# Routing of the second expert stage moved into retention; shared tiles and expert blocks in one program

## The chip, the cores and the metric

The kernel runs on one core of one Trainium2 chip. The metric is the device time of one execution in microseconds, the median of the runs. A core has TensorE (PE, matrix products), VectorE (DVE), ScalarE (ACT), GpSimd (POOL) and SyncE (SP, which here only issues transfers). Each engine works through its own instruction list in order, and they meet at semaphores.

## What is computed

4096 tokens (16 sequences of 256) with 128 channels pass through six residual stages:

```python
    x = x + 0.5 * _L0_ffn_ref(_layernorm(x, axis=-1), ...)
    x = x + _L0_attn_ref(_layernorm(x, axis=-1), ...)
    x = x + 0.5 * _L0_ffn_ref(_layernorm(x, axis=-1), ...)
    x = x + 0.5 * _L1_ffn_ref(_layernorm(x, axis=-1), ...)     # experts, first time
    x = x + _L1_attn_ref(_layernorm(x, axis=-1), ...)          # retention, 8 heads
    x = x + 0.5 * _L1_ffn_ref(_layernorm(x, axis=-1), ...)     # experts, second time
    return x
```

Retention projects q, k, v and a gate, rotates q and k, multiplies the scores by a fixed decay instead of a softmax, normalises each head's output, gates it and projects it back. The expert stage:

```python
        topk_idx, tw = _route(x, router_w, bias)   # sigmoid, 2 of 4 groups by their two best, 4 of 16 experts
        combine = (jax.nn.one_hot(topk_idx, E, dtype=tw.dtype) * tw[..., None]).sum(1)
        h = jnp.einsum('td,edf->etf', x, gate_w)
        u = jnp.einsum('td,edf->etf', x, up_w)
        y = jnp.einsum('etf,efd->etd', jax.nn.silu(h) * u, down_w)
        routed = jnp.einsum('etd,te->td', y, combine)
        sh = jax.nn.silu(x @ sh_gate_w) * (x @ sh_up_w) @ sh_down_w   # shared experts, every token
        return (routed + sh).reshape(hidden_states.shape)
```

## The kernel before

The residual `x_res` stays in SBUF as 32 tiles of 128 tokens. The stages are separate programs (`nc.Block`), one after the other. In each, every engine has a list that code writes out; there is no scheduler.

**Retention** (`retention_phase`) works in 64 steps, a pair of heads of one sequence each, so four steps make a sequence. `software_pipeline` is given, for each engine, its operations with a lead: in step s an operation with lead 3 works on pair s + 3. The order in that list is the order in the step. It runs as a loop on the engines, except for its first and last steps. PE does in a step: scores, projection of q and k (`project_qk`), `retain` (decayed scores by values), `project_v` (into the bank `ps_b`), `transpose_heads`, `project_gate`, `project_out`. Once a sequence it transposes the next one's normalised x (`transpose_x`, L1743, also into `ps_b`). DVE does: `shift_of_head`, `decay`, `turn` (L1615, rotation products), `head_statistics`, `gate_heads` (z, L1645); and for a sequence the split of x, residual, normalisation (L1601), statistics, and the adding back of the first expert stage's rows. POOL adds the rotated halves (`rotate`, L1669), without which the next scores can't start.

**The second expert stage** is `moe_phase`: `moe_route`, then `moe_blocks`, both 32 tiles or 37 blocks long and written out.
`moe_route` first runs through all 32 tiles in groups of four: statistics on DVE, inverse deviation on POOL, normalisation on ACT (into `rows`), transposes and router products on PE. Then come 32 tiles of the shared experts (`gate_up`, silu on ACT, `multiply` on DVE at L626, `transpose_act`, `down`; once in four tiles DVE's `add_shared` (L632) empties the bank that `down` fills). Between the multiplications DVE works on the choice of experts (`topk`), for 16 tiles of tokens at a time, four small operations after each tile:

```python
            for s in range(SEGS):
                for i in range(0, TOPK, 4):
                    topk(s, i, i + 4)
                    shared(done, done + 1)
                    done += 1
                classes(s)
                weights_of_row(s)
```

PE counts the rows of each class (`rank_tokens`), POOL scatters each tile's rows to DRAM (`slots`, L679), and DVE fills a table of blocks. `moe_blocks` then takes 37 blocks of 128 rows that share a pair of expert groups, computes their eight experts, and scatters the results (`y_rows`), which are read back and added at the end.

## Time and profile before

| what | value |
|---|---|
| three runs | 1536.6 us median, 1534.93 to 1537.35 |
| the profiled execution | 1533.22 us, of which the span in the trace is 1531.4 us |
| busy in the span | PE 88%, DVE 63%, ACT 52%, POOL 40% |
| mean granted TensorE clock | 0.943 of full speed |

The profile is of one execution. "Busy" counts the engine's computing; an engine that holds at a semaphore is idle. Behind an arrow stands what ended the idle time before an instruction. Retention fills about 775 to 1185 us of the span, the second routing and shared tiles 1185 to 1299 us, the second blocks 1300 to 1513 us.

### The profile page before, as it was taken

The page shows a single profiled execution, that of the slowest core. Times are in us where ns is not written, and L with a number is a line of the kernel's source. Part 1 is how long each engine was busy: PE and PEld are TensorE (multiplying, and loading weights), DVE is VectorE, ACT ScalarE, POOL GpSimd, SP SyncE. Part 2 cuts the span into 40 slices and gives each one's busy share as a digit, 9 for nine tenths or more (in the row PEclk, how much of TensorE's full clock was granted, in tenths as well). Part 3 has the DMA queues.
Part 4 walks back from the last instruction along what each step waited for, and adds up shares of the span by engine and source line. Part 5 has one row for each costly group of instructions (what it writes and reads, how often), then busy time and mean ns, then how long its engine had stood idle before and what let it go on. Part 6 is the DMA issues. An engine that isn't in the chain of part 4 may idle for free. (4 is left out here: it accounts for less than half of the span.)

```text
span 1531.4 us, 36438 instructions
## 1 busy us (share of the span) xinstructions
PE 1349.6 (88%) x10678; PEld 1139.4 (74%) x10678; DVE 968.9 (63%) x3998; ACT 790.5 (52%) x1899; POOL 609.3 (40%) x905
## 2 busy tenths in 40 slices
PE   6799999999766679999969999999997766999994
PEld 5577777776754568888858888888887445888884
DVE  6467777775766735555547777777776683555553
ACT  2267777777244234444336666666665622344441
POOL 2177777776250622222124444444443244111111
PEclk9899999999658899999979999999999788999998
DMA  5399300000220100000012121111210001000004
GB/s 142 87 296 277 104 0 0 0 1 2 98 88 17 45 30 25 27 27 25 23 49 49 47 51 48 46 48 48 51 41 22 1 31 34 24 27 25 27 27 121
DMA packets 101068, 81.59 MB, mean 53 GB/s; under 512 B 10060, under 2 KB 88591, under 8 KB 100704
## 3 DMA queue, kind: packets, MB, share of 16 engines
q1 hardware_dynamic: 95162, 68.82, 16.7%
q0 software_dynamic: 4416, 9.58, 1.8%
q10 hardware_dynamic: 1382, 1.83, 0.4%
q8 instruction: 58, 0.95, 0.3%
q14 instruction: 50, 0.41, 0.1%
HBM read 22.67 MB, written 40.75 MB: 41 GB/s over the span
## 5 line engine op out<-in xcount | busy, mean ns | idle before, releaser
L912 DVE SCALAR_TENSOR_TENSOR moe_block_act<-banks,moe_taken,moe_block_gated 128x128 f32<-128x128 f32 x592 | 166.8, 344 | 188.7 <-ACT moe_block_gated L956 180.7
L941 POOL DMA_INDIRECT y_rows<-moe_block_y,moe_taken x74 | 71.3, 963 | 366.5 <-ACT moe_block_y L966 366.5
L1231 POOL TENSOR_TENSOR attn_z<-attn_top,attn_z 128x256 f32<-128x256 f32 x256 | 155.7, 617 | 60.1 <-DVE attn_top L1178 60.1
L1178 DVE CUSTOM_DVE_ANT_0 attn_z<-banks,rel_bias 128x128 f32<-128x128 f32 (+1 forms) x512 | 148.5, 352 | 42.2 <-PE banks L1326 40.8
L956 ACT ACTIVATE moe_block_gated<-banks 128x512 f32<-128x512 f32 x148 | 88.6, 599 | 160.4 <-PE banks L997 160.3
L1669 POOL TENSOR_TENSOR ret_rotated<-ret_turned 128x512 f32<-128x512 f32 x64 | 82.1, 1283 | 189.5 <-DVE ret_turned L1615 189.5
L1013 PE MATMUL banks<-moe_down,moe_block_actT 128*128 x1184 | 156.3, 275 | 0.0
L1013 PEld LDWEIGHTS banks<-moe_down,moe_block_actT 128*128 128x128 f32 x1184 | 143.8, 192 | 0.3
L995 PE MATMUL banks<-moe_hi,moe_block_x_hi 128*128 x296 | 130.9, 442 | 1.7 <-DVE moe_block_x_lo L902 1.5
L1712 ACT ACTIVATE ret_normed<-banks,ret_head_shift,ret_head_rstd 128x128 f32<-128x128 f32 x256 | 96.4, 457 | 56.7 <-DVE ret_head_shift L1639 56.7
L1264 ACT ACTIVATE attn_prob<-banks 128x384 f32<-128x384 f32 x256 | 119.2, 492 | 7.2 <-PE banks L1336 2.4
L997 PE MATMUL banks<-moe_hi,moe_block_x_lo 128*128 x296 | 118.2, 399 | 0.0
L996 PE MATMUL banks<-moe_lo,moe_block_x_hi 128*128 x296 | 117.9, 398 | 0.0
L1336 PE MATMUL banks<-ident,attn_z 128*128 128x128 f32 x768 | 109.1, 278 | 0.7 <-ACT attn_prob L1264 0.7
L679 POOL DMA_INDIRECT slots<-moe_rows,moe_row_i x64 | 62.7, 979 | 106.1 <-issue 53.9
L1336 PEld LDWEIGHTS banks<-ident,attn_z 128*128 128x128 f32 x768 | 84.3, 141 | 14.4 <-issue 13.9
L1004 PE MATMUL banks<-ident,moe_block_act 128*128 128x128 f32 x592 | 89.1, 273 | 0.0
L1732 PE MATMUL banks<-ret_x_hi,ret_hi 128*128 128x256 f32 x256 | 84.5, 330 | 0.9 <-DVE ret_x_lo L1608 0.9
L1004 PEld LDWEIGHTS banks<-ident,moe_block_act 128*128 128x128 f32 x592 | 71.7, 141 | 17.1 <-DVE moe_block_act L912 0.2
L1615 DVE TENSOR_TENSOR ret_turned<-ret_twins,ret_cos_sin 128x1024 f32<-128x1024 f32 x64 | 77.8, 1215 | 6.1 <-DMA ret_twins<-ret_twins 6.0
L1621 DVE TENSOR_TENSOR ret_decayed<-banks,ret_decay 128x768 f32<-128x768 f32 x64 | 61.2, 956 | 30.6 <-PE banks L1788 29.9
L1645 DVE TENSOR_TENSOR ret_z<-ret_affine,ret_gate 128x512 f32<-128x512 f32 x64 | 44.3, 693 | 55.1 <-ACT ret_affine L1721 55.1
(264 smaller groups left out, 3637.5 us busy)
## 6 DMA issues: line engine op xcount, KB each, us to landing
slots<-moe_pad SPq DMA_DIRECT2D x12, 2304.0 KB, 19.9
ret_twins<-ret_twins SPq DMA_DIRECT2D x256, 64.0 KB, 2.0
moe_taken<-slots SPq DMA_DIRECT2D x74, 72.0 KB, 1.8
moe_stage<-in_moe_w SPq DMA_DIRECT2D x4, 576.0 KB, 6.6
bias_reversed<-scratch SPq DMA_DIRECT2D x1, 2048.0 KB, 9.9
back_of_seq<-y_rows SPq DMA_DIRECT2D x16, 128.0 KB, 2.2
moe_back<-y_rows SPq DMA_DIRECT2D x8, 256.0 KB, 4.9
out<-x_res SPq DMA_DIRECT2D x8, 256.0 KB, 4.2
```

What stands on the lines that cost most here:

```text
L912: last = dve.scalar_tensor_tensor(act_f[:, i, at], ps_u[:, i, at], taken[:, b % RB, column:column + 1], gated[:, i, at], ALU.mult, ALU.mult)
L956: act.activation(gated[:, k % 2, :], ps_h[:, k % 2, :], ACT.Silu).then_inc(gated_ready, 1)
L995: pe.matmul(out, hi, w_hi[:, bass.ds(at, HALF)], start=True, stop=False)
L996: pe.matmul(out, hi, w_lo[:, bass.ds(at, HALF)], start=False, stop=False)
L997: pe.matmul(out, lo, w_hi[:, bass.ds(at, HALF)], start=False, stop=True).then_inc(ready, 1)
L1004: last = pe.transpose(ps_a[:, i, e * P:(e + 1) * P], act_f[:, i, e * P:(e + 1) * P], ident[:, :])
L1013: last = pe.matmul(ps_y, actT[:, i, e * P:(e + 1) * P], w["down"][:, bass.ds(at + e * C, C)], start=(i == 0 and e == 0), stop=(i == 1 and ...
L1178: last = dve.tensor_tensor_reduce(out=z[:, s, cols], in0=ps_s[:, i, cols], in1=bias, scale=1.0, scalar=-3.0e38, op0=ALU.add, op1=ALU.max, ...
L1231: pool.tensor_tensor(z[:, s, P:WIDTH], top[:, s, 1:2].to_broadcast([P, WIDTH - P]), z[:, s, P:WIDTH], ALU.subtract).then_inc(shifted1, 1)
L1264: act.activation(prob[:, slot(k, i), :], ps_p[:, i % 2, 0:WIDTH], ACT.Exp, scale=-1.0).then_inc(prob_ready, 1)
L1336: last = pe.transpose(ps_p[:, i % 2, j * P:(j + 1) * P], z[:, s, j * P:(j + 1) * P], ident[:, :])
L1712: last = act.activation(normed[:, r, i, :], ps_o[:, r, i * RET_V:(i + 1) * RET_V], ACT.Identity, bias=head_shift[:, r, i:i + 1], scale=hea ...
```

## The change

A class `RouteFront` holds the routing of the second stage. Its work is now put between the operations of retention, behind the sequence that it needs: in step 4(q+1) the statistics of sequence q (whose residual is then complete), inverse deviation on POOL and, one step later, the normalisation, now on POOL too; two steps after that the transposes on PE, and two further on the router. Router logits come straight out with tokens on partitions (`x_hi` as the stationary operand, 16 columns), so the transposes of logits go. The choice is made for 10, 12 and 10 tiles: the first in steps 26 to 39, the second in steps 50 to 59, the third in the shared tiles. A segment is now 48 operations on DVE, each waiting for the one before. 14 of the 32 scatters are issued on POOL in retention. Front operations on PE use `ps_b` too, so `project_v` waits until they are read out.

Retention is written out in full (`every_step`) instead of looped. Its `turned` tile is gone: the products are written over `twins`, and the copy of q and k waits for `rotated_ready` instead of `turned_ready`. The `retire` (clearing of semaphores and a barrier) that stood between retention and the second expert stage now stands before retention.

`moe_tail_phase` is one program for the 32 shared tiles and the 37 blocks. It transposes and splits the stored normalised rows again for the shared experts, a group ahead. The last sequence's front and the last segment's choice run among its tiles.

```diff
+FRONT_SEGMENTS = ((0, 10), (10, 12), (22, 10))
+class RouteFront:
+    RANK_AT, ROW_AT, OPS = 35, 43, 48
...
+    def normalise(self, pool, q):
+        pool.wait_ge(self.rstd_done, q + 1)
+        for j in range(BATCH_TILES):
+            t = q * BATCH_TILES + j
+            last = pool.tensor_scalar(self.rows[:, t, 0:C], self.x_res[:, t, :], self.mv[:, q % 2, j, 0:1], self.rstd[:, q % 2, j:j + 1],
+                                      ALU.subtract, ALU.mult)
+        last.then_inc(self.xn_ready, 1)
...
+    def router(self, pe, q, ps):
+        r_hi, r_lo = self.w["router"]
+        pe.wait_ge(self.x_split, q + 1)
+        for j in range(BATCH_TILES):
+            hi, lo = self.x_hi[:, j * P:(j + 1) * P], self.x_lo[:, j * P:(j + 1) * P]
+            out = ps[:, j * MOE_E:(j + 1) * MOE_E]
+            pe.matmul(out, hi, r_hi, start=True, stop=False)
+            pe.matmul(out, hi, r_lo, start=False, stop=False)
+            last = pe.matmul(out, lo, r_hi, start=False, stop=True)
+        last.then_inc(self.routed, 1)
...
 def retention_phase(...)
+    RANKS = {40: 0, 60: 1}
+    SIGMOIDS = {25: 0, 49: 1}
+    CHOICES = {0: (26, 40), 1: (50, 60)}
+    SCATTERS = {step: (step - 42,) for step in range(42, 52)} | {62: (10, 11), 63: (12, 13)}
...
-                wait_free(dve, rotated_ready, pair(it, k, 2))
-                dve.tensor_tensor(turned[:, k % 2], twins[:, k % 2], w["cos_sin"][:, :, :].unsqueeze(2).to_broadcast(shape), ALU.mult).then_inc(turned_ready, 1)
+                dve.tensor_tensor(twins[:, k % 2], twins[:, k % 2], w["cos_sin"][:, :, :].unsqueeze(2).to_broadcast(shape), ALU.mult).then_inc(turned_ready, 1)
...
+            every_step(-9, STEPS, U, [
+                (1, shift_of_head), (0, front_statistics), (3, decay), (0, front_choice(0)), (0, front_aggregate), (6, per_seq(0, split_x)),
+                (0, front_split), (0, front_rows), (4, turn), (0, front_choice(1)), (2, head_statistics), (0, front_choice(2)),
+                (1, gate_heads), (0, front_choice(3)),
                 (0, per_seq(RET_PAIRS - 1, residual)), (7, per_seq(0, normalise_x)), (8, per_seq(0, layernorm)), (9, per_seq(0, add_back))])
...
+            every_step(-8, STEPS, U, [
+                (4, rotate), (2, inverse_head_std), (8, per_seq(0, inverse_std)), (0, front_std), (0, front_normalise), (0, front_scatter)])
...
+            every_step(-6, STEPS, U, [
+                (1, normalise_heads), (6, per_seq(0, copy_x_hi)), (0, front_copy), (5, copy_plain), (5, copy_value), (1, scale_heads), (3, silu_gate),
+                (0, front_sigmoid)])
...
@@ project_v
+                step = it * U + k - 5
+                if step % 4 == 3 and step >= 7:
+                    pe.wait_ge(front.x_split, (step - 7) // 4 + 1)
+                if step % 4 == 1 and step >= 9:
+                    pe.wait_ge(front.logits_ready, (step - 9) // 4 + 1)
...
+            every_step(-6, STEPS, U, [
+                (0, front_job), (6, per_seq(0, transpose_x)), (3, scores), (5, project_qk), (2, retain), (5, project_v), (1, transpose_heads),
                 (3, project_gate), (0, project_out)])
...
+def moe_tail_phase(...):
+            for t in range(TILES):                       # DVE
+                g = t // GROUP
+                multiply(t)
...
+                if t % GROUP == 1 and 2 <= g + 1 < GROUPS:
+                    split_x(g + 1)
+                if t % GROUP == 2 and t > GROUP:
+                    add_shared(g - 1)
+                if 4 <= t < RANK_TILE:
+                    front.choose(dve, LAST, (t - 4) * 4, (t - 3) * 4)
+                elif t == RANK_TILE:
+                    front.choose(dve, LAST, (t - 4) * 4, front.OPS, ps_rank)
```

On DVE, in retention, this is what a step holds. Before, a step of the loop in which the next sequence's x is normalised (`shift_of_head` at L1639 to z at L1645, then `ret_xn`):

```order
L1639 SCALAR_TENSOR_TENSOR ret_head_shift<-ret_head_mv,ret_head_rstd 128x4
L1619 REGISTER_ALU
L1621 TENSOR_TENSOR ret_decayed<-banks,ret_decay 128x768
L1615 TENSOR_TENSOR ret_turned<-ret_twins,ret_cos_sin 128x1024
L1627 BN_STATS ret_head_stats<-banks 128x6 x4
L1632 BN_AGGR ret_head_mv<-ret_head_stats 128x2 x4
L1527 REGISTER_ALU
L1645 TENSOR_TENSOR ret_z<-ret_affine,ret_gate 128x512
L1601 TENSOR_SCALAR ret_xn<-x_res,ret_mv,ret_rstd 128x128 x2
```

After, DVE again, step 50, the first of the second segment's choice (tiles are named `front_`; 192 elements are 12 tiles of 16 experts):

```order
L2336 SCALAR_TENSOR_TENSOR ret_head_shift<-ret_head_mv,ret_head_rstd 128x4
L2318 TENSOR_TENSOR ret_decayed<-banks,ret_decay 128x768
L1231 TENSOR_SCALAR front_not_low<-front_logits 128x192
L2306 TENSOR_TENSOR ret_x_lo<-banks,ret_x_hi 128x256
L2312 TENSOR_TENSOR ret_twins<-ret_twins,ret_cos_sin 128x1024
L1232 RECIPROCAL front_inv_l<-front_logits 128x192
L2324 BN_STATS ret_head_stats<-banks 128x6 x4
L2329 BN_AGGR ret_head_mv<-ret_head_stats 128x2 x4
L1233 TENSOR_TENSOR front_score<-front_silu_l,front_inv_l 128x192
L2342 TENSOR_TENSOR ret_z<-ret_affine,ret_gate 128x512
L1234 TENSOR_SCALAR front_tanh_l<-front_tanh_l 128x192
```

Four operations of the choice have come between retention's own, one ahead of `turn` and the last behind z.

On PE, this is what stands between the end of retention and the first matrix product of the shared tiles. Before (the first rows of the route stage; 32 transposes, 24 router products and 32 transposes of logits stand there in all, in the pattern of these rows):

```order
L1818 MATMUL banks<-ret_out_w,ret_z 128x128 x8
L1471 UNCONDITIONAL_BRANCH
L745 UNCONDITIONAL_BRANCH
L751 MATMUL banks<-ident,moe_rows 128x128 x8
L759 MATMUL banks<-moe_x_hi,router_hi 16x512
L760 MATMUL banks<-moe_x_lo,router_hi 16x512
L761 MATMUL banks<-moe_x_hi,router_lo 16x512
L751 MATMUL banks<-ident,moe_rows 128x128 x4
```

After, PE at the same place (L2590 is retention's last projection, L1630 the first product of shared tile 0, L1172 to L1174 a sequence's router, L1153 the last sequence's transposes):

```order
L2590 MATMUL banks<-ret_out_w,ret_z 128x128 x4
L2170 UNCONDITIONAL_BRANCH
L1614 UNCONDITIONAL_BRANCH
L1620 MATMUL banks<-ident,front_rows 128x128 x8
L1630 MATMUL banks<-moe_hi,moe_x_hi 128x512
L1631 MATMUL banks<-moe_lo,moe_x_hi 128x512
L1632 MATMUL banks<-moe_hi,moe_x_lo 128x512
L1172 MATMUL banks<-router_hi,front_x_hi 128x16
L1173 MATMUL banks<-router_lo,front_x_hi 128x16
L1174 MATMUL banks<-router_hi,front_x_lo 128x16
```

The first shared tile now follows eight transposes of stored rows; the rest of the transposes for the shared experts comes four at a time among the tiles.

## Rows read from the trace of the kernel before

**Rows 1.** The page, part 1: busy us, share of the span, instructions.

```profile
PE 1349.6 (88%) x10678; PEld 1139.4 (74%) x10678; DVE 968.9 (63%) x3998; ACT 790.5 (52%) x1899; POOL 609.3 (40%) x905
```

**Rows 2.** Stretches: length, busy PE, PEld, DVE, ACT, POOL, PE clock, DMA share, GB/s.

```profile
790.00:1135.00 345.00, 332.10 (x2650) 302.66 (x2648) 259.96 (x798) 227.29 (x515) 156.92 (x197) 1.00 0.20 49
1135.00:1184.00 49.00, 43.92 (x357) 40.23 (x355) 31.66 (x97) 31.14 (x72) 18.06 (x22) 1.00 0.11 28
1184.00:1212.00 28.00, 17.58 (x86) 9.15 (x84) 16.26 (x84) 20.43 (x49) 10.54 (x18) 0.76 0.01 1
1212.00:1262.00 50.00, 33.14 (x177) 25.51 (x177) 41.91 (x201) 14.32 (x42) 15.78 (x16) 0.83 0.07 24
```

**Rows 3.** Timeline, end of retention to first block: start, length, instruction, idle before.

```profile
1184.18 0.42 DVE L1650 TENSOR_TENSOR x_res<-banks,x_res 128x256 f32<-128x256 f32 x1 [1.25 <-PE banks L1818]
1185.98 0.11 DVE L441 MEMSET moe_masked<- 128x64 f32 x1 [1.37 <-PEq L57]
...
1212.43 0.50 PE L790 MATMUL banks<-moe_hi,moe_x_hi 128*128 128x512 f32 x1
...
1220.91 0.48 PE L790 MATMUL banks<-moe_hi,moe_x_hi 128*128 128x512 f32 x1
...
1302.87 0.79 PE L995 MATMUL banks<-moe_hi,moe_block_x_hi 128*128 x1 [0.77 <-DVE moe_block_x_lo L902]
```

**Rows 4.** Waits, 800 to 1150 us: us in total, times, longest.

```profile
DVE ret_z L1645 <- ACT ret_affine L1721: 47.4, 57, 0.9
DVE ret_decayed L1621 <- PE banks L1788: 25.2, 29, 1.4
PE banks L1743 <- DVE ret_xn L1601: 12.4, 14, 1.0
```

**Rows 5.** Timeline of PE in retention.

```profile
953.88 0.28 PE L1733 MATMUL banks<-ret_x_lo,ret_hi 128*128 128x256 f32 x1
953.99 0.28 PE L1734 MATMUL banks<-ret_x_hi,ret_lo 128*128 128x256 f32 x1
...
962.33 0.43 PE L1743 MATMUL banks<-ident,ret_xn 128*128 128x128 f32 x2 [0.97 <-DVE ret_xn L1601]
```

**Rows 6.** Timeline of POOL, PE and DVE in retention.

```profile
953.07 1.29 POOL L1669 TENSOR_TENSOR ret_rotated<-ret_turned 128x512 f32<-128x512 f32 x1 [3.20 <-DVE ret_turned L1615]
...
955.45 0.70 PE L1786 MATMUL banks<-ret_rotated 64*128 64x256 f32 x4
...
963.66 0.96 DVE L1621 TENSOR_TENSOR ret_decayed<-banks,ret_decay 128x768 f32<-128x768 f32 x1 [1.40 <-PE banks L1788]
```

**Rows 7.** Timeline of DVE, first operation of a 16-tile choice, and the end.

```profile
1238.30 0.41 DVE L487 TENSOR_SCALAR moe_not_low<-banks 128x256 f32<-128x256 f32 x1
...
1260.05 0.42 DVE L626 TENSOR_TENSOR moe_gated<-banks,moe_gated 128x256 f32<-128x256 f32 x1
```

**Rows 8.** Groups on DVE, 1238.3 to 1260 us: busy, mean ns, idle before.

```profile
L626 DVE TENSOR_TENSOR moe_gated<-banks,moe_gated 128x256 f32<-128x256 f32 x8 | 3.4, 420 | 3.0 <-ACT moe_gated L718 2.8
L632 DVE SCALAR_TENSOR_TENSOR x_res<-banks,x_res 128x512 f32<-128x512 f32 x2 | 1.4, 681 | 0.0
```

**Rows 9.** Timeline of PE: sixteen rank products stand between these two.

```profile
1235.31 0.21 PE L776 MATMUL banks<-moe_hot,moe_rank 128*128 128x96 bf16 x1
...
1235.79 0.47 PE L790 MATMUL banks<-moe_hi,moe_x_hi 128*128 128x512 f32 x1
```

**Rows 10.** Timeline of PE, shared tiles: `down` of a group's first tile.

```profile
1287.05 0.68 PE L807 MATMUL banks<-moe_down,moe_actT 128*128 128x128 f32 x4 [1.40 <-DVE x_res L632]
...
1294.14 0.68 PE L807 MATMUL banks<-moe_down,moe_actT 128*128 128x128 f32 x4 [1.40 <-DVE x_res L632]
```

**Rows 11.** Three lines on POOL: count, shortest/median/longest ns, first and last start.

```profile
L1230 POOL TENSOR_TENSOR attn_z<-attn_top,attn_z x128: 396/401/412, 78.9 to 376.3; 128x128 f32<-128x128 f32 x128
L1664 POOL TENSOR_TENSOR ret_rstd<-ret_var_eps,neg_half x16: 712/716/727, 774.4 to 1129.5; 128x2 f32<-128x2 f32 x16
L1675 POOL TENSOR_SCALAR ret_head_var<-ret_head_mv x64: 225/228/538, 796.6 to 1177.4; 128x4 f32<-128x4 f32 x64
```

686 lines of the change are left out of this document (662 added, 24 removed).

## The prediction

> **What bounds the kernel now.** I read the page first: PE is busy 88% of the span [rows 1], so the question is where PE is not working and what would fill it. The table by stretches answers. In retention PE is busy 332.1 of 345 us at full clock; in the first part of the second expert stage, 1184 to 1212 us, 17.6 of 28 at a clock of 0.76, and from 1212 to 1262 us 33.1 of 50, with DVE at 41.9 [rows 2]. So retention is bound by PE, and the route stage by chains between engines and then by DVE. The timeline gives its length: retention's last residual ends at 1184.18 + 0.42 = 1184.60, and the first weight product of a block starts at 1302.87 [rows 3]. Those 118.3 us are what the change can shorten.
>
> How much room is in retention is in the waits. DVE waits in 350 us 47.4 us for ACT's affine output, 57 times, and 25.2 us for scores, and PE 12.4 us for the normalised x in 14 places, once a sequence [rows 4]. I counted a period of 24.65 us for a sequence (14 of them are the 345 us), of which DVE waits 72.6/14.2 = 5.1 us. A part of that is of no use to the choice: right after PE's wait for x, DVE stands 1.40 us before `decay` [rows 6], and in the new order no operation of the choice stands between xn and `decay`.
>
> **The change, part by part.**
>
> *The route stage ends, and the tail begins.* Gone from the path are the group-wise layer norm, normalisation and router. What stays ahead of shared tile 0 is the end of one program and start of the next, 1.4 us (1184.60 to 1185.98) [rows 3], then eight transposes, two copies, the last sequence's statistics and two splits, five links of 0.3 to 0.7 us (nearest row: 0.68 for 512 elements on DVE [rows 8]): 2.6 us, together 4.0. Tiles 0 to 3 took 1220.91 - 1212.43 = 8.5 us [rows 3]; they lose the choice but gain two routers and a pair of transposes: 8.5 again. For tiles 4 to 13 I need the price of the choice. At 16 tiles its 32 steps run from 1238.30 to 1260.05, 21.75 us [rows 7], less seven multiplications (3.0), two additions (1.4) and 2.8 of waits [rows 8]: 14.6 us. The 16 operations behind them are mostly narrow, about 0.24 us each: 3.8, together 18.4. An operation takes 0.42 us at 256 elements and 0.68 at 512 [rows 8], so about 0.16 is fixed; and the maximum, match and reciprocal steps scale with tiles. At 10 tiles that gives 13.5 us, at 12 tiles 15. In the tail: 40 of 48 operations are 11.3 us in ten tiles, 1.13 each; DVE also has 0.34 for `multiply`, and a quarter each of an addition and a split (0.3): 1.8 us, and the same wait as before of about 0.35 plus some cold PE: 2.3 a tile, 23. Tile 14, with the last eight and the rank: 3.5. Without a choice a group of four takes 1294.14 - 1287.05 = 7.09 us [rows 10]; four transposes on PE ahead of it (4 x 0.12) make 7.6, 1.9 a tile. Tiles 15 to 20 carry the table, 2.2 each: 13; tiles 21 to 31, 21. Drain 3.0, then the first block's transpose, copy and split 1.1: its rows are in SBUF, since POOL has its last ten scatters out by about 55 us. Sum: 4.0 + 8.5 + 23 + 3.5 + 13 + 21 + 4.1 = 77. Gain: 118.3 - 77 = 41 us. Bounds: all tiles at 1.9 give 69 (gain 49); tiles 4 to 14 at the 2.7 that 16-tile operations cost, and a cold PE, give 86 (gain 32).
>
> *PE in retention.* Fourteen routers of six products are added. No row shows one with 16 columns. Its stationary operand is the same 128x128 as in the projections, where products of 256 columns follow each other at 0.11 to 0.12 us [rows 5]; that is the upper end, the lower is the 0.03 of the rank products (sixteen in 0.48 us) [rows 9]. I take 0.11, since the load of the stationary operand stays: 14 x 6 x 0.11 = 9.2 us (2.5 to 10). Fifteen pairs of transposes at 0.25 (0.22 to 0.36, the pair of row 962.33 took 0.36 with its start): 3.8. Two ranks of 11 and 13: 0.9. Together 14 us, all on the path, since PE has nothing to give. The wait for x stays: it comes from DVE's z and xn, which come after the same `project_v`.
>
> *DVE in retention.* Each sequence gets two statistics, two aggregations and a split, 1.2 us. Outside the choice steps DVE then needs 24.65 - 5.1 + 1.2 = 20.8 of about 25.6 us: hidden. Whether it makes PE late is a question of `turn`: its product must pass POOL's `rotate` (953.07 to 954.36) before the scores at 955.45, 1.1 us of slack [rows 6]. The statistics put 0.8 us in front of `turn`: just hidden. In steps 26 to 39 the 43 operations of the first segment cost 12.6 us, 3.6 a sequence: 20.8 + 3.6 + 1.4 of unusable wait = 25.8 against 25.6. Level; single operations of over 1 us ahead of `turn` will miss the slack now and then: 2 us. In steps 50 to 59 43 operations of 12 tiles, 14 us, are 5.6 a sequence: 27.8, so DVE becomes the bound, 2.2 x 2.5 sequences = 5.5, with lumps 7.
>
> *Banks and drain.* `project_v` waits for DVE's split and ACT's copy of logits. Both copies on ACT stand behind its four normed heads, which by my count end shortly before `project_v` begins: 0 to 0.4 us in 29 places. I take 2 in all. Steps 60 to 63 are a latency chain already (PE 43.9 of 49 [rows 2]): rank, row numbers and a router in it, 2.5. Retention grows by 14 + 2 + 7 + 2 + 2.5 = 27.5 us. Bounds: 10 (small routers, DVE all hidden) and 50.
>
> *At nothing.* POOL: normalisation, 2 x 0.4 us [rows 11], inverse deviations and scatters; it is busy 45% in retention [rows 2] and they stand behind `rotate` in the step. If that cover went, `rotate` would be late by up to 1.3 us. The wait of the q and k copy on `rotated_ready` is met early: `rotate` of the step before ends at 954.36, ahead of the scores of 955.45 [rows 6], and the copy comes behind the projection that follows those. On SP nothing is moved past the swaps. The `retire` moves ahead of retention, beside the 2 us of a read that is waited for anyway. The loop's end costs nothing now that could be won.
>
> A page speaks against it. DVE's `turn` and z have two SBUF inputs, and POOL gets instructions that read SBUF. On POOL the addition of epsilon takes 228 ns, but 538 at the longest of 64 [rows 11], so something does collide, rarely. The Trainium skill ("SBUF — State Buffer", Who interferes with whom) says that such a DVE instruction contends with a GpSimd instruction that reads SBUF, and whoever comes second blocks fully. By the row the new POOL operations cost nothing, by the rule up to their own length; the trace agrees that it happens, not that it is common.
>
> **Sum.** The profiled execution of 1533.2 - 41 + 27.5 = 1519.7 us. The median is 3.4 us above that execution: 1523.
>
> **Rivals.**
> *A. It goes as summed*: 1523, from 1512 to 1532.
> *B. The front hides well.* The choice fits in DVE's waits, the routers cost 0.03 each, the tail runs at the group's pace: -49 + 12 gives 1500. For it: DVE waits 5.1 us a sequence. Against: 1.4 of that are out of reach, and DVE was already what made the shared tiles slow.
> *C. Retention loses the order of its steps.* DVE, in order, makes `turn` late by an operation in each choice step and by the statistics once a sequence, `rotate` follows, and PE, the bound, stands. At 1 us in 24 choice steps and in 15 others it is 39 us, with PE's 14 and the drain 55, against a gain of 41 or less: 1550. It decides from an average stall of some 0.7 us a step upwards; below that the change still gains. For it: slack of 1.1 us only. Against: stalls overlap with the wait for x that PE has anyway.
> *D. POOL and DVE block each other.* New POOL operations that read SBUF are 0.23 + 0.7 + 2 x 0.4 = 1.7 us a sequence [rows 11]; if each holds up DVE in full, 16 x 1.7 = 27 us more: 1550. The page just named would have it so.
> *E. No effect*: gain and growth cancel within 3 us: 1536.6.
>
> **How the numbers follow.** A measurement of this kernel tells 0.2% (3 us) from nothing. Chances: A 0.52, B 0.18, C 0.17, D 0.05, E 0.08. A and B are faster, with a little of C's lower end: 0.72; same 0.08; slower 0.20. The likeliest is A, 1523, by itself 1512 to 1532. The range goes from B's near end, 1502, to 1543, leaving out the far ends of B, C and D.
>
> **What the profile after would show.** Retention, from its first transpose to the last residual, 436 instead of 409 us; a sequence 25.6 us outside the choice, 28 in steps 50 to 59, with PE's added idle time before scores and ended by `rotate`. From the last residual to the first block's product 77 instead of 118 us. Router products 0.11 us apart. DVE busy about the same in all (the choice is moved, not removed), its waits in retention half of before. The prediction is wrong if a sequence without choice takes over 27 us, if the shared tiles 4 to 13 take over 28 us or under 19, or if blocks wait for scattered rows.

## The result, and the profile after

The changed kernel takes 1523.7 us (median of 7 runs, 1520.4 to 1529.1); the kernel before, run beside it, 1536.6. The ratio is 0.9916, 95% interval 0.9887 to 0.9944: faster by 0.8%. 1523 was forecast. The profiled execution spans 1522.0 us (1523.8 in all), against 1531.4. The page's first part, which answers to [rows 1], shows that the gain is in how the work overlaps: PE has 7 us more to do, DVE 8 and POOL 59, and only ACT has less, by 11.

```profile
PE 1356.5 (89%) x10736; PEld 1156.0 (76%) x10736; DVE 976.9 (64%) x4056; ACT 779.6 (51%) x1893; POOL 668.1 (44%) x953
```

The same stretches as in [rows 2], at the places they have now (the columns are those of [rows 2]): retention's body, its end, and the tail in two halves. In retention's body PE is as full as before (96%), DVE went from 75 to 80% and POOL from 45 to 62%; behind it PE is busy 77% throughout, where it had begun with 17.6 of 28.

```profile
799.80:1159.00 359.20, 343.12 (x2748) 313.23 (x2748) 287.53 (x952) 230.69 (x541) 222.30 (x256) 1.00 0.20 50
1159.00:1215.48 56.48, 47.46 (x388) 42.67 (x388) 41.69 (x175) 32.27 (x77) 31.22 (x37) 1.00 0.11 27
1215.48:1255.00 39.52, 30.36 (x152) 25.52 (x153) 21.72 (x90) 13.14 (x37) 11.09 (x13) 0.78 0.06 20
1255.00:1296.41 41.41, 32.01 (x195) 26.37 (x195) 20.25 (x56) 14.44 (x42) 9.57 (x10) 0.92 0.08 26
```

The timeline gives the borders, as [rows 3] did:

```profile
774.46 0.27 ACT L967 COPY moe_block_y<-banks 128x128 f32<-128x128 f32 x1 [2.32 <-PE banks L1014]
784.01 0.69 PE L2508 MATMUL banks<-ident,ret_xn 128*128 128x128 f32 x2 [9.59 <-DVE ret_xn L2299]
...
1215.06 0.42 DVE L2347 TENSOR_TENSOR x_res<-banks,x_res 128x256 f32<-128x256 f32 x1 [0.92 <-PE banks L2590]
1215.27 0.96 POOL L1329 DMA_INDIRECT slots<-front_rows,front_row_i  x1 [0.30 <-issue]
1218.47 0.48 DVE L1123 BATCH_NORM_STATS2 front_stats<-x_res 128x6 f32<-128x128 f32 x2 [2.98 <-PEq L2170]
...
1296.41 0.49 PE L1687 MATMUL banks<-moe_hi,moe_block_x_hi 128*128 x1 [0.95 <-DVE moe_block_x_lo L1499]
```

From these: retention, 784.01 to 1215.48, takes 431.5 us, 22.7 more than 408.7 (forecast 27.5 more). From the last residual to the first block product it is 80.9 us instead of 118.3 (forecast 77). Blocks take 206.2 us instead of 209.2 from their first product to PE's last. And retention starts 8.2 us later: 1.0 in the gap ahead of it (9.59 instead of 8.62), 7.2 because the first expert stage, whose code is the old one, ended at 774.4 instead of 767.2. The sum is 22.7 - 37.3 - 3.0 + 8.2 = -9.4, the difference of the two spans.

The 7.2 us are not the change's. In both profiles TensorE ran at its lower level (1.2 GHz, granted 0.5) from 385 us on, in the feed-forward stage ahead of the first expert stage. Before, it rose at about 405 (1.00 from 410 to 420) and fell again at 425; after, it rose only behind 430, though PE was busy throughout. The first expert stage began 2.9 us later (its first transpose at 452.71 instead of 449.80), and it took 4.5 us longer.

```profile
410.00:420.00 10.00, 10.00 (x48) 9.78 (x47) 6.81 (x40) 1.54 (x4) 2.53 (x4) 0.50 0.00 0
420.00:430.00 10.00, 10.00 (x48) 9.56 (x46) 6.12 (x29) 3.41 (x8) 1.49 (x3) 0.50 0.01 2
```

From its first transpose to its first block product the first expert stage took 108.8 us in the profile of before and 113.3 here; with the same code three later profiles had 113.1 to 113.3 and eight on two other chips 128.4 to 130.0. So lengths of stages, not spans, carry the argument below.

Inside retention, I read the distance between the transposes of successive sequences (the first of them at 784.01, the last at 1158.96). Before: 24.56 and 24.74 in turn. After: 25.29 to 25.32 in the sequences with no choice; 25.94, 25.56, 27.32, 25.89 under the first segment's choice; 25.98 and 26.97 under the ten scatters; 27.63 where the second choice begins; and 56.5 from the last transpose to the last residual, against 49.9. One sequence without a choice, PE's rows: the added transposes and the six router products, 0.11 us apart as forecast.

```profile
954.46 0.38 PE L1153 MATMUL banks<-ident,front_rows 128*128 128x128 f32 x2
954.77 0.70 PE L2558 MATMUL banks<-ret_rotated 64*128 64x256 f32 x4
...
966.25 0.26 PE L1172 MATMUL banks<-router_hi,front_x_hi 128*128 128x16 f32 x1
966.36 0.26 PE L1173 MATMUL banks<-router_lo,front_x_hi 128*128 128x16 f32 x1
966.47 0.26 PE L1174 MATMUL banks<-router_hi,front_x_lo 128*128 128x16 f32 x1
...
966.99 0.70 PE L2558 MATMUL banks<-ret_rotated 64*128 64x256 f32 x4
```

One thing in these sequences is not the choice's. Behind PE's wait for x of 1.79 us TensorE's granted clock fell to 0.50 for some 3 us, in the middle of a stage that is at 1.00 otherwise. The columns are those of [rows 2]; the first line is the whole sequence in which the second choice begins.

```profile
1131.33:1158.96 27.63, 26.30 (x198) 23.95 (x198) 23.57 (x79) 16.63 (x39) 19.65 (x22) 0.94 0.18 47
1132.20:1135.20 3.00, 3.00 (x17) 2.72 (x16) 2.25 (x4) 2.35 (x6) 2.47 (x3) 0.50 0.00 0
```

```profile
1131.33 0.44 PE L2508 MATMUL banks<-ident,ret_xn 128*128 128x128 f32 x2 [1.79 <-DVE ret_xn L2299]
...
1133.86 0.41 PE L2498 MATMUL banks<-ret_x_lo,ret_hi 128*128 128x256 f32 x1
1134.07 0.41 PE L2499 MATMUL banks<-ret_x_hi,ret_lo 128*128 128x256 f32 x1
```

Products stand 0.21 us apart there, which are 0.11 apart in a sequence without a choice. Laid beside such a sequence, PE loses 1.5 us between 1132.3 and 1135.6, of the 2.3 by which this one is longer. And DVE, whose 23.57 us of work are in the first line, is idle for 4.1 of its 27.6.

The waits of 808 to 1159 us answer to [rows 4]: DVE's waits for affine and scores fell from 72.6 to 40.7 us, PE's wait for x did not fall, and DVE now waits for POOL.

```profile
DVE ret_z L2342 <- ACT ret_affine L2474: 21.8, 41, 0.9
DVE ret_decayed L2318 <- PE banks L2560: 18.9, 24, 1.3
...
PE banks L2508 <- DVE ret_xn L2299: 13.4, 14, 1.8
DVE ret_head_shift L2336 <- POOL ret_head_rstd L2410: 12.5, 34, 1.0
```

### The profile page after: what moved, and what is told of

The parts are those of the page before. It is cut to its first block and busy times, and to the rows that moved or that the text cites. A ratio compares the mean times of both kernels' runs of the same rounds, so it can differ in the third digit from the quotient of the medians.

```text
span 1522.0 us, 36111 instructions
## 1 busy us (share of the span) xinstructions
PE 1356.5 (89%) x10736; PEld 1156.0 (76%) x10736; DVE 976.9 (64%) x4056; ACT 779.6 (51%) x1893; POOL 668.1 (44%) x953
## 3 DMA queue, kind: packets, MB, share of 16 engines
q1 hardware_dynamic: 95162, 68.82, 16.9%
## 5 line engine op out<-in xcount | busy, mean ns | idle before, releaser
L2402 POOL TENSOR_TENSOR ret_rotated<-ret_twins 128x512 f32<-128x512 f32 x64 | 82.3, 1286 | 146.9 <-DVE ret_twins L2312 146.8
L2030 PEld LDWEIGHTS banks<-ident,attn_z 128*128 128x128 f32 x768 | 84.6, 141 | 14.4 <-issue 13.8
L2312 DVE TENSOR_TENSOR ret_twins<-ret_twins,ret_cos_sin 128x1024 f32<-128x1024 f32 x64 | 77.6, 1212 | 6.1 <-DMA ret_twins<-ret_twins 5.9
L2410 POOL TENSOR_TENSOR ret_head_rstd<-ret_head_var,neg_half 128x4 f32<-128x4 f32 x64 | 76.0, 1187 | 5.3
L2499 PE MATMUL banks<-ret_x_hi,ret_lo 128*128 128x256 f32 x256 | 72.8, 285 | 0.0
L2498 PE MATMUL banks<-ret_x_lo,ret_hi 128*128 128x256 f32 x256 | 72.7, 284 | 0.0
L1707 PEld LDWEIGHTS banks<-moe_down,moe_block_actT 128*128 128x128 f32 x592 | 71.9, 192 | 0.1
```

Source lines behind the costliest of these rows:

```text
L1707: last = pe.matmul(ps_y, block_actT[:, i, e * P:(e + 1) * P], w["down"][:, bass.ds(at + e * C, C)], start=(i == 0 and e == 0), stop=(i == ...
L2030: last = pe.transpose(ps_p[:, i % 2, j * P:(j + 1) * P], z[:, s, j * P:(j + 1) * P], ident[:, :])
L2312: dve.tensor_tensor(twins[:, k % 2], twins[:, k % 2], w["cos_sin"][:, :, :].unsqueeze(2).to_broadcast(shape), ALU.mult).then_inc(turned_re ...
L2402: pool.tensor_tensor(rotated[:, k % 2], twins[:, k % 2, 0], twins[:, k % 2, 1], ALU.add).then_inc(rotated_ready, 1)
```

## The experiments

Twelve kernels in four groups, beside the kernel before, on three chips: shell to load_late on one, after_again to add_first on the second, the last four on the third. Before took 1572.7 and 1569.4 us on the first two of them and 1538 to 1540 on the third; ratios are to it on the same chip. The changed kernel itself did not run on the third: paced stands in for it there.

**shell**: the kernel before in the form of the changed one, with no work moved.

```
-            software_pipeline(dve, BATCHES // GU, U, [
+            every_step(-9, STEPS, U, [
-                dve.tensor_tensor(turned[:, k % 2], twins[:, k % 2], ...)
+                dve.tensor_tensor(twins[:, k % 2], twins[:, k % 2], ...)
+            retire(nc, used)
             retention_phase(nc, "ret", ...)
-        retire(nc, used)
```

> The kernel before with only the shell of the change: retention written out step by step instead of in a loop, the product of turn written in place into twins, and the release of semaphores ahead of retention instead of behind it; no work is moved. My theory, that all of retention's growth (22.7 us, first transpose to last residual, 408.7 before) comes from the front's own instructions, expects retention at 408.7 within 1 us, with 24.65 us for a sequence, and the first transpose of retention 9.3 to 9.6 us behind the last product of the first expert stage, as after (9.59) instead of 8.62: so 1 us later, and the total within 2 us of before. The rival, that longer straight code or the buffer in place costs in every step, expects part of the 0.66 us that a sequence grew by, that is 3 to 10 us in retention. A third point: the end of retention to the next program's first instruction on DVE, 1.37 us before and 2.98 after. If written-out code makes that edge long, it is near 3 here; if POOL's scatters at the end do, it stays at 1.4.

Ratio 0.9978 (0.9948 to 1.0008). Retention 408.2 us; sequences 24.56 to 24.57, all of them, where before had every second one at 24.74 with PE's wait at 0.97 instead of 0.80. So the end of the loop's body had cost 0.17 us, 1.1 us over retention, which I had put at nothing; retention as a whole fell by only 0.6, since its end took 50.4 us instead of 49.9. The gap ahead of retention is 9.33 us: releasing the semaphores there costs 0.7, and the other 0.25 of the change are the pads. The edge behind retention fell to 0.37 us from 1.38, without the release and without scatters. All growth of retention is the front's own: 431.5 - 408.2 = 23.3.

**router_one**: one product for each tile instead of three.

```
-            pe.matmul(out, hi, r_hi, start=True, stop=False)
-            pe.matmul(out, hi, r_lo, start=False, stop=False)
-            last = pe.matmul(out, lo, r_hi, start=False, stop=True)
+            last = pe.matmul(out, hi, r_hi, start=True, stop=True)
```

> The changed kernel with one product for each tile in the front's router instead of three (hi by hi alone; the two corrections are left out, so the logits are coarser and a token may choose other experts). It takes 56 products of 16 columns out of retention (14 batches by 4). My theory, that PE's instruction stream sets retention's length and that each of them takes its 0.113 us (rows 966.25 to 966.81) on the path, expects a sequence without choice at 25.31 - 0.45 = 24.86 us and retention at 431.4 - 6.3 = 425. The rival, that a sequence is set by the chain through DVE and POOL to the normalised x (PE waits 0.8 us for it in each), and products only fill time, expects the wait to grow by what is taken out, a sequence at 25.2 to 25.3 and retention at 430 or more. The tail gives back under 1 us in both.

Ratio 0.9884 (0.9836 to 0.9932). Sequences without choice 25.0 instead of 25.3, the wait for x still 0.80 (one of the five stayed at 25.31): 0.31 of the 0.45 us taken out came back. PE's stream is on the path there, as my theory has it. But retention stayed at 431.7, so the 6 us forecast did not come. In the four sequences of the first choice nothing came back (104.7 us together, as in the changed kernel). The second choice's first sequence took 29.3 us instead of 27.6, and that says nothing of the router: the same sequence takes 29.32 in paced, whose retention is the changed kernel's line for line. Both have a collision there, shown with the rivals below.

**scatter_late**: no scatter in retention.

```
-    SCATTERS = {step: (step - 42,) for step in range(42, 52)} | {62: (10, 11), 63: (12, 13)}
+    SCATTERS = {}
-FRONT_BEHIND = 14
+FRONT_BEHIND = 0
...
+            front.await_rows(pool, 0)
```

> The changed kernel with none of the 14 scatters in retention: all 22 rows of the first two segments are scattered by POOL in the tail. My theory is that scatters on POOL cost twice: 2.3 us in the two sequences of steps 42 to 51 (25.98 and 26.97 us against 25.31 without them, PE waiting 1.49 and 1.79 us for x), and that the four in the last two steps hold the end of the program, since POOL's last one ends at 1216.23, 0.75 us behind the last residual. So: those sequences at 25.3, the edge from last residual to DVE's first instruction at 2.2 or less instead of 2.98, in all 3 to 4 us less. The rival for the edge, the length of code or the jump to it, expects 3.0 there again. What speaks against a gain at the other end: 22 scatters of 1.26 us, and their start behind the normalisation, reach to 1249, before the last ten are ready at 1260, so blocks are not late. If they are, the first block product comes later than 81 us after the last residual.

Ratio 0.9913 (0.9887 to 0.9939). The two sequences went to 25.29 and 25.28, and the edge from 2.99 to 0.32 us:

```profile
1243.77 0.42 DVE L2348 TENSOR_TENSOR x_res<-banks,x_res 128x256 f32<-128x256 f32 x1 [1.33 <-PE banks L2591]
1244.51 0.49 DVE L1123 BATCH_NORM_STATS2 front_stats<-x_res 128x6 f32<-128x128 f32 x2 [0.32 <-PEq L2171]
```

Both were as expected; the rest was not. Retention as a whole came to 430.7 us, only 0.8 less: the two sequences gave 2.4 back and the clock stayed at 1.00 behind them, but the next one has the collision shown below (28.15 us), and the end took 0.9 longer. The profiled execution took 1575.5 us, the longest of the five, whose median is 1559.8. Its tail took 104.2 us, against 82.1 to 91.1 in the other kernels with the front on the two slow chips, with one hole of 13 us in which PE, DVE and ACT all stood while POOL scattered; by the median, most executions will not have had such a hole. PE's products for the tile were done at 1264.2; ACT's silu of them started at 1275.47:

```profile
1262.09 0.37 ACT L1564 COPY moe_actT<-banks 128x256 f32<-128x256 f32 x1 [1.74 <-remote]
1275.47 0.38 ACT L1559 ACTIVATE moe_gated<-banks 128x256 f32<-128x256 f32 x1 [13.01 <-remote]
```

```profile
1248.45 1.10 POOL L1329 DMA_INDIRECT slots<-front_rows,front_row_i  x1 [0.17 <-issue]
...
1275.12 0.95 POOL L1329 DMA_INDIRECT slots<-front_rows,front_row_i  x1 [0.31 <-issue]
```

**load_late**: blocks' rows are read only when the shared tiles are added.

```
             sync.wait_ge(front.scattered, TILES * 16)
+            sync.wait_ge(shared_added, GROUPS)
```

> The changed kernel with one wait more: SP reads the first block's rows only when the last group of shared tiles is added, as the end of a program between shared tiles and blocks would have it. It takes back what one program for both gives. My theory: before, PE waited 3.7 us for the first rows; so the first block product comes 3.5 to 4.5 us later, the tail at 84.5 to 85.5 us instead of 80.9, and the total 4 us over that of the changed kernel. The rival, that the merged program gives nothing since the rows arrive within the last chain of products and additions, expects under 1 us.

Ratio 0.9890 (0.9859 to 0.9921). PE waits 3.6 us for the first rows, a wait which before had at 3.7 and after does not have; blocks took 207.5 instead of 206.4 us, with TensorE's clock at 0.92 in their first 17 us instead of 1.00. These two, 4.7 us, are what one program for shared tiles and blocks gives. The tail took 91.1 us, 4.6 more than in router_one on the same chip, but ACT stood still at other places in the two, so that this difference alone would not show it.

```profile
PE banks L1679 <- DMA moe_taken<-slots: 3.6, 1, 3.6
```

**after_again**: the changed kernel on the second chip.

> The changed kernel as it is, on the chip and in the rounds of the next three, since the chip of the last four runs was 2.3% slower for the kernel before (1572.7 us). Both theories expect the same of the stages: retention 431.5 within 1 us, with sequences of 25.3 us without choice, 25.9, 25.6 and 27.3 in the first segment's steps, 26.0 and 27.0 under the scatters. My theory says that retention, which PE sets at full clock, repeats to 1 us on any chip, and that what differs from run to run lies in the expert stages: the last product of the first expert stage, 767 us in the profile of before and 774 in that of after, from code that the change leaves alone. The rival, that this 7 us belongs to the change, expects a ratio of about 0.988 on a chip of the first kind only if that product comes 7 us later than in a kernel with the old code.

Ratio 0.9866 (0.9803 to 0.9929). Retention 431.8 us, every sequence within 0.2 us of the first profile. Not every profile repeats so well: the six that have the changed kernel's retention (this one, after, load_late, add_first, add_split, paced) have 431.5 to 433.9 us, and 27.5 to 29.3 for the sequence in which the second choice begins. So a difference in retention of up to 2 us between two profiles need not be an edit's. The first expert stage took 129.7 us, as in the shell with the old code on the third chip (129.7): what differs between chips and profiles lies there.

**points**: the choice's operations at other places in DVE's order.

```
-  (0, front_statistics), (3, decay), (0, front_choice(0)), ... (1, gate_heads), (0, front_choice(3)),
+  (0, front_statistics), (0, front_choice(0)), (3, decay), ... (1, gate_heads), ...
+  (9, per_seq(0, add_back)), (0, front_choice(3))
```

> The changed kernel with the choice's operations at other places of DVE's order in retention: those that stood behind decay stand ahead of it, where DVE waits for the scores (23.8 us in 27 places in all), and those between z and the normalised x stand behind x, for which PE waits. The same operations in the same steps. My theory, that the choice costs retention because single operations stand in front of work that PE waits for (the first segment's four sequences took 25.94, 25.56, 27.32 and 25.89 us against 25.3, that is 3.5 us, the second's first one 27.63), expects about half of that back: the first four at 25.5 on the mean, 2.5 less, and retention at 427 to 429. The rival, that DVE is simply full there, expects retention within 1 us of 431.5, since the work is the same. It would be worse, over 433, if a long operation ahead of decay (reciprocal 1.12, match 1.4 us) makes scores and retain late.

Ratio 0.9875 (0.9839 to 0.9911). The first four sequences came to 25.72, 25.47, 26.74, 25.79, 1.0 us less together, not 2.5 (the six profiles above have 104.7 to 105.5 for the four, this one 103.7); the second choice's first one took 29.13 instead of 27.5, with the same collision as router_one and paced; retention 431.3. So the place is worth something under the first choice, less than half of my forecast. That DVE is full, as the rival has it, is not shown: in the changed kernel it is idle for 3.4 to 4.7 us in each of these four sequences, and for 5.7 of the 29.1 us here.

**spread**: segments of 10, 10, 12, and the second choice in 14 steps.

```
-FRONT_SEGMENTS = ((0, 10), (10, 12), (22, 10))
+FRONT_SEGMENTS = ((0, 10), (10, 10), (20, 12))
-    CHOICES = {0: (26, 40), 1: (50, 60)}
+    CHOICES = {0: (26, 40), 1: (46, 60)}
```

> The changed kernel with segments of 10, 10 and 12 tiles instead of 10, 12 and 10, and the second one's choice over the 14 steps 46 to 59 instead of ten. My theory, that in steps 50 to 59 the choice makes DVE the bound (27.63 us for the sequence in it, and 56.5 for the end of retention against 50.4 without any front), expects 3 to 4 us back in retention, 427.5 to 428.5, and gives 1.5 us away in the tail, whose choice has 12 tiles: in all 2 us less than the changed kernel beside it. The rival, that the end of retention is long because of what is in its last four steps (rank, row numbers, router, scatters), expects the end at 56 again and retention at 430 to 431, so with the tail 1 us more in all.

Ratio 0.9838 (0.9776 to 0.9900). Retention 430.0 instead of 431.8, its end 54.6 instead of 57.0, the second sequence under scatters, which now has choice too, 0.8 longer; the tail 86.5 instead of 84.6. What went here came back there: inconclusive as to total, and at most half of my 3 to 4 us in retention.

**add_first** and **add_split**: the addition of a group earlier in DVE's order (the split's line unchanged in add_first, as below in add_split).

```
+                if t % GROUP == 2 and t > GROUP:
+                    add_shared(g - 1)
                 multiply(t)
-                if t % GROUP == 1 and 2 <= g + 1 < GROUPS:
+                if t % GROUP == 2 and 2 <= g + 1 < GROUPS:
                     split_x(g + 1)
-                if t % GROUP == 2 and t > GROUP:
-                    add_shared(g - 1)
```

> The changed kernel with the addition of a group of shared tiles to the residual one place earlier in DVE's order in the tail: ahead of the multiplication of tile 4g+2 instead of behind it. PE's first down product of each group waits for it, 13.7 us in seven places of the tail (up to 3.2 us each), and the addition itself waits for a multiplication that needs PE and ACT first. My theory, that this order and not DVE's load sets the pace of a group in the tail (7.1 us for four tiles at full clock, of which 1.4 are this wait), expects the wait at 2 to 5 us and the tail 8 to 11 us shorter, the total 0.6% below the changed kernel. The rival, that the chain through silu, multiplication, transpose and copy sets a tile's pace anyway, expects the wait to move to the transposes or the copies and a gain under 3 us.

> As the run before with the earlier addition, and now the split of the next group's x (DVE, 0.69 us, which itself waits 0.33 us for ACT) stands behind the multiplication of tile 4g+2 instead of ahead of the addition. In the last run the wait of PE's down product for the addition was 0.2 us where no split stood ahead of it and 1.06 where one did, against 1.40 in the old order. My theory expects all the waits in tiles without choice at 0.2 us and the group at 6.0 us instead of 7.1, the tail 5 to 7 us shorter than the changed kernel's (80.9 us on the first chip, 84.6 on the second). The rival, that DVE's choice and ACT's late starts decide, expects no more than the 2 us that the earlier addition alone gave.

The first: ratio 0.9819 (0.9778 to 0.9860), the tail 82.1 us against 84.6 beside it, far from the 8 to 11 forecast. Where a split stood ahead of the addition, PE's wait went only from 1.40 to 1.06 us. The second: 0.9845 (0.9797 to 0.9893) on the quicker chip, the tail 67.7 us, against 80.9 in the changed kernel and 80.8 in the next one on the same chip. That is more than the 5 to 7 us expected: a group of four went from 7.10 us (1284.33 to 1291.43 after) to 6.17 and 5.72 (below), and the groups with a choice gained too.

```profile
1265.67 0.68 PE L1647 MATMUL banks<-moe_down,moe_actT 128*128 128x128 f32 x4
...
1271.84 0.68 PE L1647 MATMUL banks<-moe_down,moe_actT 128*128 128x128 f32 x4
...
1277.56 0.68 PE L1647 MATMUL banks<-moe_down,moe_actT 128*128 128x128 f32 x4
```

**paced**: one scatter for each tile in the tail.

```
             for t in range(FRONT_BEHIND, FRONT_SEGMENTS[LAST][0]):
+                pool.wait_ge(gated_ready, t - FRONT_BEHIND + 1)
                 front.scatter(pool, t)
...
             for t in range(FRONT_SEGMENTS[LAST][0], TILES):
+                pool.wait_ge(gated_ready, t - FRONT_SEGMENTS[LAST][0] + RANK_TILE + 2)
                 front.scatter(pool, t)
```

> The changed kernel with one wait more ahead of each of the 18 scatters in the tail: POOL may issue one for each tile of the shared experts (it waits for ACT's silu of that tile), instead of all of them one behind the other. On the slower chips ACT stood still for 1 to 7 us several times, and once for 13 us, with its operands ready, and each time inside a row of scatters (in the run with all scatters in the tail from 1262.5 to 1275.5 us, 22 scatters from 1248.5 to 1276.1); in retention, with one scatter a step, no such stop is seen. My theory, that it is the dense row of scatters that holds ACT up, expects the stops of over 1 us to go and the tail 3 us shorter on a slower chip, unchanged on a chip like the first. The rival, that the stops belong to the straight code of the tail whatever POOL does, expects them to stay. Last rows are out by tile 25, so blocks start as before in both.

Ratio 0.9914 (0.9879 to 0.9948), tail 80.8 us. It ran on the quicker chip, where no kernel shows a stop of ACT to begin with, so no change was expected there. Inconclusive.

**best** and **best_both**: the order of add_split, the waits of paced and the edits below; then the earlier addition in the first expert stage too.

```
-    SCATTERS = {step: (step - 42,) for step in range(42, 52)} | {62: (10, 11), 63: (12, 13)}
+    SCATTERS = {step: (i,) for i, step in enumerate((42, 43, 45, 46, 47, 49, 50, 51, 53, 54))}
-FRONT_BEHIND = 14
+FRONT_BEHIND = 10
...
+            front.await_rows(pool, 1)
...
-            front.set_pads(dve)
+            def front_pads(it, k):
+                if it * U + k == 1:
+                    front.set_pads(dve)
...
+                (0, front_pads), (1, shift_of_head), ...
```

> What the runs point to, in one kernel: the earlier addition with the split behind it; scatters paced, one a tile; the ten scatters of retention not in the steps in which POOL has the front's inverse deviation (42, 43, 45 to 47, 49 to 51, 53, 54 in place of 42 to 51), and the four of the last two steps moved to the tail; the pads set in step 1 instead of ahead of retention. By the parts: 5 to 6 us from the addition, 2.3 less the rest for sequences under scatters (25.98 and 26.97 to 25.3 and 25.6), 2.3 at the edge (2.7 to 0.4), 0.25 from the pads: 9 to 11 us below the changed kernel, a ratio of 0.985 on a chip of the first kind and 0.98 or less on a slower one. The rival, that some of these only move a wait (DVE full in the tail, POOL late for the last rows), expects half of it.

> The best kernel so far, with the earlier addition in the first expert stage too, whose code is that of the kernel before. There PE waits 14 to 16 us for the addition in five or six places, and the old second stage has the same (16.8 in seven). My theory, that this order costs in both stages wherever tiles run without choice, expects the waits in the first stage at half or less and the stage 6 to 8 us shorter, the ratio to before at 0.975 instead of 0.980. It also says what the same edit would have given the old kernel: about that much in each of its two stages, so that the change would gain about as much on top of it as without. The rival, that with 16 tiles to a choice DVE is behind in tiles 0 to 13 anyway, expects under 4 us, since only the tiles after the table gain.

Ratios 0.9796 (0.9750 to 0.9841), 1507.2 us, and 0.9746 (0.9692 to 0.9799), 1497.9 us: 2.5% below the kernel before, the intervals clear of the changed kernel's 0.9887 to 0.9944 above and of paced's on this chip. In best the sequences under scatters are 25.31 and 25.31, the edge 0.32, the gap ahead of retention 9.33, the tail 61.9 us. In best_both the first expert stage took 106.6 us, against 113.3 in three profiles on that chip, the 6 to 8 expected, though only 2.2 under the 108.8 of before's profile; and PE's wait for the addition went only from 16.9 to 11.6 us, not to half. So the total is measured, the size of this piece is not settled.

## Why the prediction was right

**The stage's end and the tail: 41 forecast, 37.3 measured.** The sum's terms, by the starts of the tiles' first products: start 5.5 (4.0 forecast), tiles 0 to 3 9.1 (8.5), tiles 4 to 13 24.5 (23), tile 14 3.9 (3.5), tiles 15 to 20 14.5 (13), the rest with drain and first block 23.5 (25.1). Start, tiles 4 to 13 and tiles 15 to 20 each took 1.5 us more than I had, the rest 1.6 less. Of these the start is explained. I took the 1.4 us between programs over; it is 3.0, and the cause is the scatters in retention's last two steps: nine profiles with them have 2.1 to 3.0, the three without (scatter_late, best, best_both) 0.32. POOL's last one ends at 1216.23, but its rows land at 1217.57, 2.3 us behind the issue, and the packed trace has the instruction that closes POOL's program running until 1218.19; the next program begins at 1218.47. In pricing the moved step I had counted its scatters under "at nothing" with POOL's busy share as cover, and no cover lies behind the last step. PE's pace in the late tiles rested on [rows 10] and their wait of 1.40 us for the addition; I took that wait as given in the term of 1.9 a tile. add_split shows it was the order of two instructions on DVE.

**Retention: +27.5 forecast, +22.7 measured.** By pieces against the shell: 12 sequences at 0.74 us are 8.9; the first choice 3.5 (2 forecast); the scatters 2.3 (0); the second choice's first sequence 2.3 and the end 6.1 (7 and 2.5); 0.2 in the first sequences; and -0.6 from the shell's form.

*PE and banks* (14 and 2 forecast, which include a part of the end). The place was right, the size somewhat large. Laid beside a sequence of the shell, PE's work starts 0.22 us later behind the two transposes and 0.57 later behind the six router products, and nowhere else; I had 0.25 and 0.66. The banks' 2 were about right, though not spread out: in the sequences without a choice PE has no wait but that for x; its waits for the front's split and logits are 1.6 us in four places up to 1159 us and 1.1 in two in the end.

*DVE as the bound in steps 50 to 59* (7). This is the step that was wrong in kind, and its size came near by luck. In the sequence in which the choice begins DVE is idle for 4.1 us and PE for 1.3, and 1.5 of the 2.3 us are TensorE's lower clock behind the wait of 1.79 us. That wait comes from the scatters. So they cost 2.3 + 1.5 = 3.8 us in retention, where I had nothing, and the second choice under 1 us up to step 53. What the end's 6.1 us consist of was not taken apart; spread, with a less dense choice, has 54.6 there instead of 57.0, so the choice has a part in it.

*The sign.* I had said that PE's added idle time would stand before the scores and be ended by `rotate`. It does not: between 808 and 1159 us PE waits for x (up to 1.79 us) and, before a projection, for DVE's splits (1.2 us for the front's, 0.7 for retention's own) and the copied logits (0.4), never for `rotate`.

**At nothing.** Three of these were not: the release of semaphores ahead of retention (0.7, shell), the pads (0.25), scatters in retention (2.3, and 1.5 by the clock). One was better than nothing: the loop's edge, 1.1 us in favour. POOL's normalisation took 0.79 us a tile, not 0.4, and was hidden all the same. Blocks gained 3.0 us that I had not counted: before, PE entered them out of a wait of 3.7 us, with the clock at 0.82 in the first 17 us, after at 1.00.

**The rivals.** B, that the front hides well, fell: retention grew by twice its 12 us. C needed 0.7 us a step; the choices cost 3.5, 2.3 and at most the 6.1 of the end in 24 steps, 0.5 each at most. D is rare, but one case costs more than its own length. The first: POOL's scatter at 1127.78 made `rotate` late, so that it met z. z took 1.68 us instead of 0.69, x was late by 1 us, PE waited 1.79, and then the clock fell.

```profile
1127.78 1.10 POOL L1329 DMA_INDIRECT slots<-front_rows,front_row_i  x1 [0.18 <-issue]
...
1128.91 1.28 POOL L2402 TENSOR_TENSOR ret_rotated<-ret_twins 128x512 f32<-128x512 f32 x1
1129.07 1.68 DVE L2342 TENSOR_TENSOR ret_z<-ret_affine,ret_gate 128x512 f32<-128x512 f32 x1 [0.86 <-ACT ret_affine L2474]
1130.15 0.69 POOL L2408 TENSOR_SCALAR ret_head_var<-ret_head_mv 128x4 f32<-128x4 f32 x1
```

The Trainium skill ("SBUF — State Buffer", Who interferes with whom) says that of a DVE instruction with two SBUF inputs and a GpSimd instruction that reads SBUF the second one blocks until the first is through; these rows agree, z by `rotate` and then the addition of epsilon (0.69 instead of 0.23) by z. But only 2 of 64 z were stretched, 1.7 us in all, where D had 27. POOL pays more often: the power of `head_rstd` took over 1.19 us, instead of 1.04, in 26 of 64, and DVE waited for it 12.5 us in all, hidden except at such places.

The second case is in seven of the twelve kernels with the front, by a hair: in the sequence in which the second choice begins, z starts at most 0.02 us ahead of POOL's addition of epsilon, which then takes 0.88 to 0.95 us instead of 0.24. The power behind it, `shift_of_head` and ACT's copy of the front's x are late in turn, and PE waits 1.28 to 1.98 us for the split of that copy. Here it is in paced:

```profile
1135.76 0.68 DVE L2344 TENSOR_TENSOR ret_z<-ret_affine,ret_gate 128x512 f32<-128x512 f32 x1
1135.77 0.95 POOL L2410 TENSOR_SCALAR ret_head_var<-ret_head_mv 128x4 f32<-128x4 f32 x1 [1.29 <-DVE ret_head_mv L2331]
...
1137.88 0.16 DVE L2338 SCALAR_TENSOR_TENSOR ret_head_shift<-ret_head_mv,ret_head_rstd 128x4 f32<-128x4 f32 x1 [1.26 <-POOL ret_head_rstd L2412]
...
1140.44 0.47 PE L2499 MATMUL banks<-ret_hi,ret_x_hi 128*128 128x512 f32 x1 [1.98 <-DVE front_x_lo L1164]
```

In the changed kernel's profile z comes 0.5 us behind the addition, and nothing of this happens. With this collision the sequence takes 28.1 to 29.3 us (router_one, scatter_late, points, add_first, paced, best, best_both), without it 27.0 to 27.9 (the other five). So D was worth 2.5 us in the changed kernel's profile, the clock included, and some 4 where both cases come: far from 27, but not nothing.

The median was right within 1 us, partly by luck. Of the stages, 4 us too much gain in the tail and 5 too much growth in retention offset each other, and within retention the clock filled a term that I had given to DVE; what I had left out (1.0 ahead of retention, -3.0 in the blocks) makes the sum of stages -16.6 us, where -13.5 was forecast and the medians differ by 12.9. What is left, 3.7 us, can lie in the unchanged first expert stage, whose length differs by more than that from profile to profile; it was not pinned down.

## What to carry to other kernels

When work moves under another stage, look at that stage's last steps and at the edge behind it: nothing hides there, and here the next program began only 2 us behind POOL's last scatter instruction. When an unchanged stretch of code takes 27.5 us in one profile and 29.3 in another, find out which instructions met before you put a change in its length down to an edit; and look at the granted clock behind every new wait, also in a stage that was at full clock. A wait that repeats at the same place in every group is worth a look at the waiting engine's order before any work is moved: two operations moved in DVE's program gave 10 us beside the 14 of the whole change on the same chip (add_split and paced, 1514.1 and 1524.4 us), on top of it. And an engine that has waits left in a stretch is not its bound, however dense its work looks there.

## What was unexpected of the hardware

The granted clock can fall inside a stage in which PE is busy 96% of the time: in eight of the nine profiles with a scatter in each of steps 42 to 51 it went to 0.50 for some 3 us right behind one of PE's waits of 1.5 to 2.0 us (in add_split twice). Not every such wait brought it down (in points it stayed at 1.00 behind 1.79 and fell behind 1.98), and the usual one of 0.80 never did.

On two of the chips ACT stood still several times in the expert stages, with its operands ready, for 1 to 7 us and once for 13, and in the tails of the kernels with the front each stop of over 1.5 us began inside a row of POOL's scatters, though some ended up to 3 us behind it; on the first chip and the last the same code shows none. Scatters one a step in retention never did it. That dense scatters are the cause is argued, not shown: the kernel that paces them did not run on such a chip. It would explain a part of the 33 us by which these chips are slower. The changed kernel, with 14 scatters spread over retention, gained 1.3% there and 0.8% on the first, but the intervals overlap. An end of a loop's body costs 0.17 us on PE's path, once in every two sequences. And the moment at which TensorE was granted its higher level in an unchanged stage (405 or 430 us) moved the rest of a profile by about 3 us.
